# Masked attention over 200 items: a block's keys and its values each in one transfer, and the small loads ahead of them on the same queue

## The reference

```python
q = target_key @ W_target.T                              # 512 x 64
k = jnp.einsum('bld,ed->ble', item_keys, W_item)
v = jnp.einsum('bld,ed->ble', item_values, W_value)
scores = jnp.einsum('bd,bld->bl', q, k) / scaler         # scaler = 8
scores = scores + -100000000.0 * (1.0 - mask)
w = jax.nn.softmax(scores, axis=1)
return jnp.einsum('bl,bld->bd', w, v)                    # 512 x 64
```

## Time and profile before

| | us |
|---|---|
| median of 3 runs | 136.64 (136.59 to 137.13) |
| profiled execution | 137.14 |
| its span, first to last instruction | 135.3 |
| outside the span | 1.84 |
| TensorE busy | 76.6 (57%) |
| VectorE, ScalarE, GpSimd busy | 12.9, 7.3, 5.6 |
| HBM read | 53.04 MB, 393 GB/s over the span |

### The profile page before, as it was taken

One profiled execution on the slowest core, in us unless ns is written; L12 is line 12 of the kernel. 1 busy time (PEld: TensorE's weight loads), 2 busy tenths in 40 slices (PEclk: granted clock), 3 DMA queues, 4 the chain that ended last, 5 costly groups with the idle time before them and its releaser, 6 DMA issues.

```text
span 135.3 us, 2879 instructions
## 1 busy us (share of the span) xinstructions
PE 76.6 (57%) x1342; PEld 54.4 (40%) x1342; DVE 12.9 (10%) x46; ACT 7.3 (5%) x22; POOL 5.6 (4%) x15
## 2 busy tenths in 40 slices
PE   0002299839180592949362393949462393957981
PEld 0000164529180351528261261628362251626970
DVE  5000000340000000022000000022000000022000
ACT  0300000030000000030000000030000000030000
POOL 7500000010000000010000000010000000010000
PEclk9999999986999559595999559595999559595599
DMA  5999999999999998999999999999999999999710
GB/s 144 428 392 376 400 423 421 456 383 462 413 439 431 416 459 386 462 401 456 396 449 444 401 462 391 446 431 434 419 426 446 398 462 409 439 387 412 322 36 10
DMA packets 3771, 53.34 MB, mean 394 GB/s; under 512 B 1072, under 2 KB 1136, under 8 KB 1584
## 3 DMA queue, kind: packets, MB, share of 16 engines
q1 hardware_dynamic: 2736, 52.43, 91.8%
q10 hardware_dynamic: 1024, 0.74, 1.7%
HBM read 53.04 MB, written 0.13 MB: 393 GB/s over the span
## 4 chain that ended last, share of the span: by engine, by line
DMA 69%; PE 25%; issue 1%; ACT 1%; ACTq 1%; DVE 1%; POOL 0%; DVEq 0%
DMA key_ring<-keys 39%; DMA value_ring<-values 20%; PE ps_scores L356 13%; DMA targets_sb<-targets 11%; PE ps_context L378 6%; PE ps_context L393 3%; PE ps_query L436 1%; PE ps_small L430 1%; PE ps_query L340 1%; ACT result L233 0%; PE ps_context L387 0%; ACT expd L220 0%; ACTq L196 0%; PE ps_turn_rest L370 0%; POOL half_twice L191 0%
## 5 line engine op out<-in xcount | busy, mean ns | idle before, releaser
L356 PE MATMUL ps_scores<-key_ring,sta_query 128*32 128x200 f32 x512 | 37.5, 473 | 21.7 <-DMA key_ring<-keys 21.2
L356 PEld LDWEIGHTS ps_scores<-key_ring,sta_query 128*32 128x32 f32 x512 | 22.2, 155 | 35.8 <-DMA key_ring<-keys 22.6
L378 PE MATMUL ps_context<-value_ring,sta_full 128*32 128x128 f32 x512 | 21.9, 337 | 2.1 <-DMA value_ring<-values 2.1
L378 PEld LDWEIGHTS ps_context<-value_ring,sta_full 128*32 128x32 f32 x512 | 19.1, 139 | 4.2 <-DMA value_ring<-values 3.4
L393 PE MATMUL ps_context<-value_ring,sta_half 128*32 128x128 f32 x256 | 10.8, 294 | 0.0
L387 PE MATMUL ps_context<-value_ring,sta_eighth 128*32 128x128 f32 x32 | 3.7, 314 | 9.9 <-DMA value_ring<-values 9.9
L393 PEld LDWEIGHTS ps_context<-value_ring,sta_half 128*32 128x32 f32 x256 | 8.7, 118 | 0.2
L335 PE MATMUL ps_small<-w_query_sb 64*64 64x128 f32 x2 | 0.7, 444 | 10.9 <-DMA w_query_sb<-w_query 10.9
L233 ACT ACTIVATE result<-ps_small,inv_sum 128x64 f32<-128x64 f32 x4 | 1.3, 314 | 97.1 <-PE ps_small L430 97.1
L191 POOL COPY half_twice<-expd 128x128 f32<-128x128 f32 x4 | 1.4, 351 | 114.8 <-ACT expd L220 114.8
L387 PEld LDWEIGHTS ps_context<-value_ring,sta_eighth 128*32 128x32 f32 x32 | 1.8, 126 | 10.7 <-DMA value_ring<-values 10.7
(11 more groups left out here) (35 smaller groups left out, 26.7 us busy)
## 6 DMA issues: line engine op xcount, KB each, us to landing
key_ring<-keys SPq DMA_DIRECT2D x8, 3200.0 KB, 25.5
value_ring<-values SPq DMA_DIRECT2D x7, 3200.0 KB, 27.4
value_ring<-values SPq DMA_DIRECT2D x1, 1280.0 KB, 26.0
value_ring<-values SPq DMA_DIRECT2D x1, 1152.0 KB, 23.3
value_ring<-values SPq DMA_DIRECT2D x1, 512.0 KB, 26.8
mask_sb<-mask_rows ACTq DMA_DIRECT2D x1, 400.0 KB, 22.3
value_ring<-values SPq DMA_DIRECT2D x1, 256.0 KB, 26.9
targets_sb<-targets ACTq DMA_DIRECT2D x1, 128.0 KB, 14.3
```

The source lines that it names most:

```text
L356: last = nc.tensor.matmul(ps_scores[g * GU:(g + 1) * GU, 0:L], window(sta_query, PITCH, g, s * PAIRS_T + k), key_ring[:, s, c:c + KB], sta ...
L378: last = nc.tensor.matmul(ps_context[g * GU:(g + 1) * GU, 0:VB], window(sta_full, PITCH, g, s * PAIRS_T + k), value_ring[:, s, c:c + VB], ...
```

## The change

- `NT` and the rings go. There is one `key_tile` and one `value_tile` of 51200 bytes a row, as large together as the rings were. A block's keys are one transfer of 6.55 MB, and so are its values. The host arrays are laid out to match.
- The keys of block n wait for `s_key_used` n, which the last score matmul of a block gives. The values of block n wait for `s_value_used` n, given by the last `weigh` matmul of a block.
- `score` is called for two halves as before, with `turn_context` of the block before between them, but only the first half waits, for the whole block's keys.
- `weigh` runs once a block: eighths, halves, full. It waits for `s_sta_rest` at its start and for `s_sta_full` before the full ones. The last block's values are five pieces: eighths and halves, then 8, 5, 2 and 1 of the 16 pairs.
- `w_query` and `targets` are one load (`query_side`, 64 rows of 2560 bytes). It, the mask and `w_value_cols` are issued by SP ahead of the first keys; ScalarE issues no loads.

The diff, cut to its core:

```diff
-    CUTS = (0, 5, 7, PAIRS_T)
+    CUTS = (0, 8, 13, 15, PAIRS)
...
-        key_ring = sb("key_ring", [P, NT, KCOLS])
-        value_ring = sb("value_ring", [P, NT, VCOLS])
+        key_tile = sb("key_tile", [P, KCOLS])
+        value_tile = sb("value_tile", [P, VCOLS])
...
         @block.sync
+            sp.dma_start(query_side_sb[:], query_side).then_inc(s_query_side, 16)
+            sp.dma_start(mask_sb[:], mask_rows).then_inc(s_mask, 16)
+            sp.dma_start(w_value_twice[:], w_value_cols).then_inc(s_w_value, 16)
             for n in range(NBLK):
-                for s in range(NT):
-                    if n > 0:
-                        sp.wait_ge(s_key_used, NT * (n - 1) + s + 1)
-                    sp.dma_start(key_ring[:, s, :], keys[n * NT + s]).then_inc(s_key[s], 16)
-                for s in range(NT):
-                    if n > 0:
-                        sp.wait_ge(s_value_used, NT * (n - 1) + s + 1)
...
+                if n > 0:
+                    sp.wait_ge(s_key_used, n)
+                sp.dma_start(key_tile[:], keys[n]).then_inc(s_key, 16)
+                if n > 0:
+                    sp.wait_ge(s_value_used, n)
+                if n < NBLK - 1:
+                    sp.dma_start(value_tile[:], values[n]).then_inc(s_value, 16)
+                else:
+                    begin = 0
+                    for c, cut in enumerate(CUTS):
+                        end = FULL_AT + cut * GRP * VB
+                        sp.dma_start(value_tile[:, begin:end], values[n][:, begin:end]).then_inc(s_value_piece[c], 16)
+                        begin = end
...
         @block.scalar
-            act.dma_start(w_query_sb[:], w_query).then_inc(s_w_query, 16)
-            act.dma_start(targets_sb[:], targets).then_inc(s_targets, 16)
-            act.dma_start(mask_sb[:], mask_rows).then_inc(s_mask, 16)
-            act.dma_start(w_value_twice[:], w_value_cols).then_inc(s_w_value, 16)
...
-            def score(n, s):
-                pe.wait_ge(s_key[s], 16 * (n + 1))
-                if s == 0:
+            def score(n, pairs):
+                if 0 in pairs:
+                    pe.wait_ge(s_key, 16 * (n + 1))
...
-                last.then_inc(s_key_used, 1)
+                if PAIRS - 1 in pairs:
+                    last.then_inc(s_key_used, 1)
...
+            def weigh(n):
+                in_pieces = n == NBLK - 1
+                if in_pieces:
+                    pe.wait_ge(s_value_piece[0], 16)
+                else:
+                    pe.wait_ge(s_value, 16 * (n + 1))
+                pe.wait_ge(s_sta_rest, 3 * (n + 1))
+                if n > 0:
+                    pe.wait_ge(s_context, n)
```

More of the change, by code:

```diff
@@ L16 @@
 PAIRS = GU // 2
-NT = 2
-PAIRS_T = PAIRS // NT
 FULL = 128
@@ L30, with masked_attention_kernel @@
 MASKED = 1.0e8
-def masked_attention_kernel(nc, w_query, targets, w_value_cols, mask_rows, keys, values, out):
+def masked_attention_kernel(nc, query_side, w_value_cols, mask_rows, keys, values, out):
     B, D = out.shape
@@ L352, in score @@
                         pe.wait_ge(s_biased, n)
-                for k in range(PAIRS_T):
+                for k in pairs:
                     for g in range(GRP):
                         c = (k * GRP + g) * KB
-                        last = nc.tensor.matmul(
-                            ps_scores[g * GU:(g + 1) * GU, 0:L], window(sta_query, PITCH, g, s * PAIRS_T + k),
-                            key_ring[:, s, c:c + KB], start=s == 0 and k == 0,
-                            stop=s == NT - 1 and k == PAIRS_T - 1)
-                last.then_inc(s_key_used, 1)
+                        last = nc.tensor.matmul(ps_scores[g * GU:(g + 1) * GU, 0:L], window(sta_query, PITCH, g, k),
+                                                key_tile[:, c:c + KB], start=k == 0, stop=k == PAIRS - 1)
+                if PAIRS - 1 in pairs:
+                    last.then_inc(s_key_used, 1)
             def turn_weights(n):
@@ L373, in turn_weights @@
                     .then_inc(s_turn_rest, 1)
-            def weigh_full(s, k):
-                for g in range(GRP):
-                    c = FULL_AT + (k * GRP + g) * VB
-                    last = nc.tensor.matmul(
-                        ps_context[g * GU:(g + 1) * GU, 0:VB], window(sta_full, PITCH, g, s * PAIRS_T + k),
-                        value_ring[:, s, c:c + VB], start=s == 0 and k == 0,
-                        stop=s == NT - 1 and k == PAIRS_T - 1)
-                return last
@@ new lines, in weigh @@
+                        nc.tensor.matmul(ps_context[g * GU:(g + 1) * GU, 0:VB], window(sta_half, PITCH_H, g, h),
+                                         value_tile[:, c:c + VB], start=False, stop=False)
+                pe.wait_ge(s_sta_full, n + 1)
+                for k in range(PAIRS):
+                    if in_pieces and k in CUTS:
+                        pe.wait_ge(s_value_piece[CUTS.index(k) + 1], 16)
+                    for g in range(GRP):
+                        c = FULL_AT + (k * GRP + g) * VB
+                        last = nc.tensor.matmul(ps_context[g * GU:(g + 1) * GU, 0:VB], window(sta_full, PITCH, g, k),
+                                                value_tile[:, c:c + VB], start=False, stop=k == PAIRS - 1)
@@ L432, in _ @@
             for n in range(NBLK):
-                for s in range(NT):
-                    score(n, s)
-                    if n == 0 and s == 0:
-                        nc.tensor.matmul(ps_query[:, P:B], w_both[:], targets_sb[:, P:B], start=True, stop=True) \
-                            .then_inc(s_query, 1)
-                    if n > 0 and s == 0:
-                        turn_context(n - 1)
-                    if n > 0 and s == NT - 1:
-                        project(n - 1)
+                score(n, range(0, HALVES))
+                if n == 0:
+                    nc.tensor.matmul(ps_query[:, P:B], w_both[:], targets_sb[:, P:B], start=True, stop=True) \
+                        .then_inc(s_query, 1)
+                else:
+                    turn_context(n - 1)
+                score(n, range(HALVES, PAIRS))
+                if n > 0:
+                    project(n - 1)
                 turn_weights(n)
-                for s in range(NT):
-                    weigh(n, s)
+                weigh(n)
             turn_context(NBLK - 1)
```

99 lines of the change are left out of this document (28 added, 71 removed).

## The result

| | before | changed |
|---|---|---|
| median, us | 136.67 (136.47 to 137.13, 6 runs) | 139.64 (138.66 to 140.76, 6 runs) |
| ratio | | 1.0175, 95% interval 1.0144 to 1.0206 |
| span of the profiled execution, us | 135.3 | 138.9 |
| TensorE waits until (start of the last keys' scores), us | 114.61 | 116.17 |
| from there to VectorE's copy behind the last weigh matmul, us | 16.85 | 18.91 |

The ratio leaves out the changed kernel's two slowest executions, of which the profiled one (140.76) is one; 1.0175 x 136.67 is 139.06.

A forecast was written before the change was run, and what follows sets the result against it. The stream of keys and values was taken as the bound, with TensorE waiting. Span 135.3, plus 3.0 for the tail, less 1.1 for the stream, plus 1.84 outside: 139.0, or 138.5 us against the median; range 136.9 to 140.6.

The forecast's parts named there:

- mechanism of the tail: After the last keys land, all scores, the softmax and weigh follow in turn: 19.8 us against 16.85, 3.0 more.
- Scores behind the last keys, 8.2 us: Last block: all 128 records follow the last keys, 5.15 us at low clock, 2.92 at full, 0.15 for the transpose.
- Softmax, 3.74: Last block, scores' end to the eighths' placing: 3.74 us, no longer hidden by values, since weigh waits for s_sta_rest.
- Weigh, 7.9: Last block's weigh in one go, not stopped by values: 7.9 us, bounds 7.3 to 8.5.
- The stream, 1.1 us earlier: Delivery of the last keys: 0.9 us earlier from the head, 0.2 from larger transfers; bounds -0.5 to 2.1.
- the dip that goes with the mixing: Head, 11 to 15 us: the low rate beside targets' load, 0.82 us lost, would go with small loads in front.
- The 0.2 us for larger transfers: Whole stream: 8 transfers in place of 16 save 0 to 0.5 us, taken as 0.2.
- the prediction's own sign of being wrong: Wrong if block 3's weigh waits for the last piece, or the last keys land over 2 us from 113.5.
- the 3 that the prediction named: Last block: the last piece of values lands 3 us or more before TensorE needs it.
- The middle of the stream at no cost: One buffer per operand costs nothing: each issue is covered by the other operand's 15.24 us transfer, margin about 7 us.
- The rival of the other side: Head: last keys land early enough to give back the tail's loss, 136.1 us; chance 0.15.
- the empty queue: Middle of the stream: fastest engines finish before the next issue, six gaps up to 1 us each, 141.5 us; chance 0.06.

The follow-up runs named there:

- e3: The changed kernel with weigh doing the full matmuls of 8 pairs first, so that it starts on sta_full alone: 138.50 us, ratio 1.0122.
- after_again: The changed kernel run and profiled once more, with no edit: 139.88 us.
- f1: The changed kernel with every bulk transfer cut into two of 3.28 MB, issued together and waited for together: 140.28 us, ratio 1.0196.
- g1: The kernel before with small loads first on SP and, in the last block, waits for both key halves and for s_sta_rest ahead of weigh: 141.02 us.
- e1: The kernel before with only the changed head, query_side, mask and w_value_cols issued by SP ahead of the keys: 136.62 us, ratio 0.998.
- f2: The kernel before with one added wait, for both halves of the last block's keys ahead of its first scores: 138.07 us, ratio 1.0075.
- e2: The changed kernel with the last block's keys in two transfers with a semaphore each: 136.42 us, ratio 0.9966.
- g2: The kernel before with only query_side at the head of SP's queue, mask and w_value_cols staying on ScalarE's queue: 136.41 us, ratio 0.9977.
- h1: The changed kernel with the last block's keys in two transfers and only query_side at the head of SP's queue: 136.01 us, ratio 0.9933.

## Why the prediction was right, and where its working was not

The forecast was 138.5 us with 136.9 to 140.6, and slower with 0.80. 139.64 lies in the range and the sign is right, and so is the mechanism of the tail. But the nearness of the number is in part luck, since two errors of opposite sign met in it. Its terms:

- **Scores behind the last keys, 8.2 us: right.** 8.15, half of it at a granted clock of 0.57 and 2.92 us at the full one, as block 0 had shown.
- **Softmax, 3.74: right.** 3.72, and weigh began 0.11 us behind VectorE's last placing, with its values long there. e3 gives the moved wait its price, 0.7 to 1.1.
- **Weigh, 7.9: 0.9 too long.** It was 7.02. The working set it between block 1's 7.3 and block 3's 8.49, for the same idleness ahead. After 3.3 us at 0.58 the clock was full, and a run of 128 full matmuls without a pause takes 3.68 us. In the sum the tail became 2.05 longer (2.4 in after_again), not 3.0. f1, in the same order, took 8.34, and g1, in the order of before, 8.5, so that the early full clock isn't a property of the order, and 7.9 was a fair value between what comes.
- **The stream, 1.1 us earlier: wrong, in sign too.** In the two profiles the last keys came 1.6 and 0.6 us later. The step that failed is the head. Its gain, the dip that goes with the mixing, is real (e1: 442 GB/s). Its loss was taken at up to 0.5 us for what the small loads leave empty. The issues took 0.42 to 0.56 us each, so that the first keys were issued at 2.50, not 2.1, and their first packets began at 4.24 in place of 1.80. The larger part is that the slowest of 16 engines decides: block 0's keys were complete at 23.50 and 22.75 in the two profiles in place of 21.11, though the fastest engine was only 0.3 us later. With this head the spread there was 1.2 to 3.3 us in nine profiles against 1.07 and 1.15, and in the bad ones the second packets were slow. The working had the spread only as something that uses up the margin. The 0.2 us for larger transfers is not borne out (f1 has none of it and is no slower than the intervals tell). By the prediction's own sign of being wrong, last keys over 2 us away from 113.5, it was wrong on the stream in the first profile (116.17) and near it in the second (115.25). The last piece of values landed at 133.06, some 1.7 us before its matmuls were due and not the 3 that the prediction named; in after_again it was 3.6.
- **The middle of the stream at no cost: right, with less margin than said.** SP's issues came 2.2 to 2.9 us before the fastest engine landed the transfer ahead, as worked out (3). The least was at 48.48, 2.17 us before. One thing cost margin that the working didn't have: in block 2, in both profiles, TensorE stood for 1.5 us within weigh, behind the same 108 records of full matmuls, with "issue" as its releaser. The rows of the changed kernel, TensorE's timeline and a stretch behind it:

```profile
108.85 0.85 PE L388 MATMUL ps_context<-value_tile,sta_full 128*32 128x128 f32 x20 [1.51 <-issue]
...
111.00:113.00 2.00, 0.00 (x0) 0.00 (x0) 0.00 (x0) 0.00 (x0) 0.00 (x0) 0.50 0.63 214
```

The last values were still issued at 109.74, 2.27 us before the fastest engine was done with the keys (112.01). The 214 GB/s are those of packets that begin in these 2 us; at no time from 111 to 113 were fewer than 14 of the 16 engines at work, and the idle time comes to under 0.1 us of all. What held TensorE is open.

The two errors, 2.2 us (the stream, between 1.1 early and 1.1 late on the mean of the two profiles) and 0.8 us (the tail), have opposite signs, so that the time came out 1.1 us above the forecast by the median and 0.6 by the ratio. The rival of the other side (the head gives back the tail) did not come; nor did the empty queue, in this kernel.

Of the 2.4 us by the ratio, f2 gives 1.0 to the wait for all keys in the last block, e3 0.7 to the wait for s_sta_rest, and 0.7 is left for the later stream; by the medians it is 3.0, 1.3, 1.1 and 0.6. The last part is a difference and wasn't measured by itself; the profiles have 0.6 and 1.6. The parts don't add up in every combination either: e2, which undoes only the first, gains 2.9 to 3.2, since with the overlap back values hide the softmax again and the moved wait costs nothing.

## What to carry to other kernels

A kernel bound by its stream can take one buffer and one large transfer for each operand in the middle, as long as each transfer is issued before the fastest DMA engine runs dry. The last block is another matter: what stands behind the last landing is the tail, and each block's unit of waiting is paid there once, so cut the last operands finely even where all others go whole, and order the work behind them by which input lands last. A stream is as late as its slowest DMA engine, so look at how evenly a head starts the 16 engines, and not only at how soon: the two kernels here with the smallest spread at the head (g2 and h1) are also, of the edited ones, those whose executions lie closest together, within 1 us.

## What the runs showed of the hardware that was not expected

- The spread of the engines lasts: 2.05 us at block 0's keys was 2.01 at block 2's keys, 60 us later (e3). Where it grew, it was in steps of 0.3 to 1.5 us; only in the changed kernel, e2 and a few others did it shrink a little (4.81 to 4.11).
- On ScalarE's queue beside bulk packets of 51200 bytes, a load of 128 KB landed at 24.0 us, with 25600 bytes at 15.7; both stood behind `w_query`, and up to there only the bulk's rows differ.
- The load of targets, 128 KB in rows of 2048 bytes, slows bulk packets beside it from 0.95 to between 1.05 and 1.43 us; 400 KB of mask in rows of 3200 bytes beside the same bulk does not (before and f2).
- 16 KB packets of the queue "instruction" run among the bulk, 10 in each profile. Each takes 0.9 to 1.1 us, and the bulk packet behind it takes about 0.5 us more.
